# A transformer decoder layer on one core: other loads for the attention row maxima and the mask, two spread steps moved from TensorE to DMA and GpSimd, and the first half's last layer norm on ScalarE

## What is computed

```python
x = layernorm(x + self_attn(x))              # 16 heads of 8, one shared K and V of width 8
x = layernorm(x + cross_attn(x, ctx, mask))  # 16 heads of 8, scores -1e9 where mask == 0
x = layernorm(x + moe(x))                    # 8 experts 128x128, top 1, times its softmax weight

def self_attn(x):
    Q = heads(x @ Wq + bq); K = x @ Wk + bk; V = x @ Wv + bv
    attn = softmax(einsum('bhsd,btd->bhst', Q, K) / sqrt(8))
    return merge(einsum('bhst,btd->bhsd', attn, V)) @ Wo + bo
```

## Time and profile before

| | |
|---|---|
| median of 3 runs | 462.83 us (462.34 to 463.98) |
| the profiled execution | 465.59 us |
| its span in the trace | 464.0 us |
| mean granted TensorE clock | 0.97 of 2.4 GHz |
| busy: PE, DVE, ACT, POOL | 94%, 85%, 78%, 54% of the span |

### The profile page before, as it was taken

One profiled execution on the slowest core, in us unless ns is written; L12 is line 12 of the kernel. 1 busy time (PEld: TensorE's weight loads), 2 busy tenths in 40 slices (PEclk: granted clock), 3 DMA queues, 4 the chain that ended last, 5 costly groups with the idle time before them and its releaser, 6 DMA issues.

```text
span 464.0 us, 10785 instructions
## 1 busy us (share of the span) xinstructions
PE 438.2 (94%) x3873; PEld 177.2 (38%) x3873; DVE 395.0 (85%) x520; ACT 360.8 (78%) x708; POOL 248.7 (54%) x383
## 2 busy tenths in 40 slices
PE   7999999999889999999999999999999999999983
PEld 2543333333334333333344334333344443333441
DVE  5969989999788899899998999999999999941455
ACT  6338888889765877788868888889968888978723
POOL 4834889987897904042456644445447354320563
PEclk9879999999988999999999999999999999999978
DMA  6957967599770056221322346322212122110000
GB/s 164 342 121 230 310 201 293 182 364 350 249 316 1 15 114 98 64 68 42 92 71 69 115 92 105 89 72 60 83 45 69 49 72 70 47 32 23 4 24 26
DMA packets 24596, 56.08 MB, mean 121 GB/s; under 512 B 6442, under 2 KB 15928, under 8 KB 22492
## 3 DMA queue, kind: packets, MB, share of 16 engines
q0 software_dynamic: 7536, 37.91, 25.1%
q1 hardware_dynamic: 16424, 17.24, 14.3%
q10 hardware_dynamic: 580, 0.20, 0.2%
HBM read 45.60 MB, written 9.18 MB: 118 GB/s over the span
## 4 chain that ended last, share of the span: by engine, by line
PE 66%; DVE 12%; POOL 8%; DMA 7%; issue 4%; ACT 2%; SPq 0%; ACTq 0%; DVEq 0%; POOLq 0%
PE O L1512 25%; PE ST L1752 15%; PE RT L1745 7%; DVE mxs L944 7%; PE ST L1539 5%; POOL big L613 4%; DMA big<-in_mask 4%; PE RT L1527 3%; PE RT L1638 2%; DMA Qs<-mxr 2%; POOL big L622 2%; PE ST L1645 1%; PE O L1490 1%; DVE mxc L962 1%; PE RT L1608 1%
## 5 line engine op out<-in xcount | busy, mean ns | idle before, releaser
L1309 ACT ACTIVATE prob<-ST 128x512 f32<-128x512 f32 x512 | 279.5, 599 | 52.0 <-PE ST L1539 21.8
L944 DVE TENSOR_REDUCE mxs<-RT 128x2 f32<-128x1024 f32 x128 | 153.2, 1222 | 17.1 <-PE RT L1527 16.2
L961 DVE TENSOR_REDUCE mxc<-RT 128x2 f32<-128x1024 f32 x128 | 152.6, 1221 | 2.8 <-PE RT L1745 1.9
L1752 PE MATMUL ST<-Qs,Kc 64*128 64x512 f32 x320 | 117.4, 450 | 0.0
L1745 PE MATMUL RT<-Kr,Qs 64*128 64x512 f32 (+1 forms) x384 | 114.5, 398 | 0.0
L1512 PE MATMUL O<-prob,vst 128*9 128x256 f32 x1280 | 99.1, 381 | 1.7 <-ACT prob L1298 0.5
L1539 PE MATMUL ST<-Qs,Kself 64*128 64x512 f32 x256 | 96.2, 448 | 2.7 <-DMA Qs<-mxr 2.6
L1527 PE MATMUL RT<-Kself,Qs 64*128 64x512 f32 x256 | 89.8, 466 | 3.2 <-DVE mxs L944 2.0
L690 POOL DMA_DIRECT2D Kr<-kd x96 | 47.9, 503 | 72.7 <-PE RT L1745 57.6
L1512 PE MATMUL O<-prob,Vs 128*9 128x256 f32 x1024 | 80.5, 386 | 1.3 <-ACT osb L1246 0.3
L1752 PEld LDWEIGHTS ST<-Qs,Kc 64*128 64x128 f32 x320 | 50.4, 184 | 66.1 <-issue 38.3
(11 more groups left out here) (224 smaller groups left out, 331.8 us busy)
## 6 DMA issues: line engine op xcount, KB each, us to landing
big<-in_mask POOLq DMA_DIRECT2D x16, 1664.0 KB, 8.0
Kc<-kd POOLq DMA_DIRECT2D x64, 80.0 KB, 2.2
Kr<-kd POOLq DMA_DIRECT2D x64, 64.0 KB, 2.1
od_s<-osb SPq DMA_DIRECT2D x16, 128.0 KB, 2.6
kd<-Vx SPq DMA_DIRECT2D x4, 512.0 KB, 6.7
Qs<-qd_x SPq DMA_DIRECT2D x8, 256.0 KB
od_x<-osb SPq DMA_DIRECT2D x14, 128.0 KB, 1.7
Qs<-qd_s SPq DMA_DIRECT2D x12, 128.0 KB, 5.6
```

The lines of the kernel that those rows point to most:

```text
L944: freed(v.tensor_reduce(mxs[:, h % 2, c2, :].rearrange("p (f t) -> p f t", f=2)[:, :, q], bank[:, :].rearrange("p (f k) -> p f k", f=2), A ...
L961: return v.tensor_reduce(o[:, :, u % 4], src, AX.X, ALU.max)
L1309: freed(nc.scalar.activation(prob[:, s % SLOTS, f * HALF:(f + 1) * HALF], bank[:, :], ACT.Exp))
L1752: mm = mmul(o[:, :], Kc[STACK[f], b * P:(b + 1) * P], Qs[STACK[f], j, :], start=True, stop=not gen, skip_group_check=True)
```

## The change

Six things are done together.

1. `split_max` makes three bfloat16 parts by four POOL operations, where two fp32r parts were made by two. PE turns 24 rows by a bfloat16 identity (`identb`) in one pass; before it turned 16 rows as fp32. The rows in `Qs` are placed elsewhere (`MAXROWS`, `PRODUCTS`).
2. The splits of heads 3, 6 and 9 move from between L613 and L622 of mask tiles 3, 7 and 12 to ahead of the waits of those tiles.
3. Each mask tile is loaded by two DMAs of half the columns.
4. For "s1" and "x0" the spread is taken off PE and DVE: SP writes `rden` to memory and reads it back widened (`inverses_out`, `inverses_in`), and POOL multiplies (`norm_work`). Their products move to X(1, 9) and X(9, 9); what follows moves by one block or one step: turn, queries, logits, router weights, normalisation, and the stores and gathers of the queries.
5. In the tail POOL normalises no tile of the first half. It makes -mean/std (`shift`), and ACT normalises the four tiles after its last expert part and before it loads the table with Sqrt. DVE's statistics of that half move from ahead of the router's operations to between the two sums of experts. POOL waits for DVE's four normalised tiles before its sums of experts, where it waited after them.
6. The turn of the second half waits tile by tile, where it waited for all four.

The diff, cut to its core:

```diff
-MAX_AHEAD = {0: 0, 2: 2, 6: 5, 9: 7, 14: 10}
-MAX_BETWEEN = {0: 1, 3: 3, 4: 4, 7: 6, 10: 8, 12: 9}
+MAX_AHEAD = {0: 0, 2: 2, 3: 3, 6: 5, 7: 6, 9: 7, 12: 9, 14: 10}
+MAX_BETWEEN = {0: 1, 4: 4, 10: 8}
...
+            def inverses_out(a):
+                k = 1 if a == "s" else 2
+                sp.wait_ge(S("rden"), k + 1)
+                load(rd[a].rearrange("u q (h k) -> (u q h) k", k=P), rden[:, :], "rden_out")
+
+            def inverses_in(a):
+                k = 1 if a == "s" else 2
+                sp.wait_ge(S("rden_out"), 16 * k)
+                for q in range(4):
+                    w, r = slice((q % 2) * 256, (q % 2 + 1) * 256), 64 * (q // 2)
+                    load(rdenw[r:r + 64, w], rd[a][:, q, :].unsqueeze(1).to_broadcast([8, DH, 256]), "rden_in")
...
-                pool.dma_start(maskI[m % 2], t["mask"][q * P:(q + 1) * P, w * HALFT:(w + 1) * HALFT]) \
-                    .then_inc(S(f"mask_in{m % 2}"), 16)
+                for c in range(0, HALFT, HALFT // 2):
+                    pool.dma_start(maskI[m % 2][:, c:c + HALFT // 2],
+                                   t["mask"][q * P:(q + 1) * P, w * HALFT + c:w * HALFT + c + HALFT // 2]) \
+                        .then_inc(S(f"mask_in{m % 2}"), 16)
...
-                g_.tensor_copy(mxh[:, :, 0, :], parts).then_inc(S("mx_part"), 1)
+                step(g_.tensor_copy(mxh[:, :, 0, :], parts))
+                step(g_.tensor_tensor(mxl[:, :, :], parts, mxh[:, :, 0, :], ALU.subtract))
+                g_.tensor_copy(mxh[:, :, 1, :], mxl[:, :, :]).then_inc(S("mx_part"), 1)
                 pool.wait_ge(S("mx_part"), G + 1)
-                g_.tensor_tensor(mxh[:, :, 1, :], parts, mxh[:, :, 0, :].bitcast(F32), ALU.subtract) \
+                g_.tensor_tensor(mxh[:, :, 2, :], mxl[:, :, :], mxh[:, :, 1, :], ALU.subtract) \
                     .then_inc(S("mx_split"), 1)
...
-                if j == 1:
+                if j in (1, 9):
+                    k = 1 + j // 8
+                    pool.wait_ge(S("o_back"), 64 * (k + 1))
+                    pool.wait_ge(S("rden_in"), 64 * k)
+                    pool.wait_ge(S("rt_ready"), number(RT_AT, ("s0 y", "s1 y")[k - 1]))
+                    g_.tensor_tensor(aT[:, :], aTr[:, :], rdenw[:, :], ALU.mult).then_inc(S("o_scaled"), 1)
...
+            pool.wait_ge(S("xn"), 16)
             upper_experts(0, 2, 4)
-            pool.wait_ge(S("xn"), 16)
...
-            for q in range(4):
-                g_.tensor_scalar(outs[:, q, :], x[:, q, :], mv[:, q, 0:1], rstd[:, q:q + 1], ALU.subtract, ALU.mult) \
-                    .then_inc(S("out0_done"), 1)
+            step(g_.tensor_tensor(shift[:, :], mv[:, 0:4, 0], rstd[:, 0:4], ALU.mult))
+            g_.tensor_scalar(shift[:, :], shift[:, :], -1.0, None, ALU.mult).then_inc(S("first_std"), 1)
...
-                if s == X(1, 3):
-                    spread_rows("s", 1)
-                if s == X(1, 5):
+                if s == X(1, 9):
                     residual("s", 1)
...
+            act.wait_ge(S("first_std"), 1)
+            for q in range(4):
+                nc.scalar.activation(outs[:, q, :], x[:, q, :], ACT.Identity, bias=shift[:, q:q + 1],
+                                     scale=rstd[:, q:q + 1]).then_inc(S("out0_done"), 1)
...
-                pe.wait_ge(S("xn"), 4 * NORMS[a, ph])
+                if (a, ph) != ("x", 1):
+                    pe.wait_ge(S("xn"), 4 * NORMS[a, ph])
                 for q in range(4):
+                    if (a, ph) == ("x", 1):
+                        pe.wait_ge(S("xn"), 13 + q)
```

More of the change, by code:

```diff
@@ L37 @@
 STACK = (slice(0, 64), slice(64, P))
-PRODUCTS = (1, 64 + 3)
-MAXROWS = slice(0, 100, 33)
+PRODUCTS = (0, 96)
+MAXROWS = slice(36, 87, 10)
 PENROWS = (34, 65)
@@ L75 @@
 RT_JOBS = {76: ("s0 spread",), 79: ("s0 y",), 94: ("count",), 99: ("flags",), KV - 1: ("km",),
-           X(1, 3): ("s1 spread",), X(1, 5): ("s1 y",), X(9, 3): ("x0 spread",), X(9, 5): ("x0 y",),
-           X(10, 6): ("x0 logits",), X(14, 6): ("e0",), X(15, 1): ("e1",),
+           X(1, 9): ("s1 y",), X(9, 9): ("x0 y",),
+           X(11, 6): ("x0 logits",), X(14, 6): ("e0",), X(15, 1): ("e1",),
            STEPS: ("x1 spread", "x1 y", "x1 logits", "e2", "e3", "u7")}
 ST_JOBS = {66: ("bias",), 86: ("s0 turn",), 88: ("s0 q",), KV: ("vm",),
-           X(2, 3): ("s1 turn",), X(2, 6): ("s1 q",), X(10, 3): ("x0 turn",),
+           X(3, 3): ("s1 turn",), X(3, 6): ("s1 q",), X(11, 3): ("x0 turn",),
            STEPS: ("c0", "u0", "u1", "b0", "u2", "u3", "x1 turn", "u4", "c1", "u5", "b1", "u6")}
@@ L251, in decoder_layer @@
         qd = {a: dram(f"qd_{a}", [2, DH, HEADS, Q]) for a in "sx"}
+        rd = {a: dram(f"rd_{a}", [8, 4, 256]) for a in "sx"}
         kd, pd = dram("kd", [HEADS, PROD, KPAD]), dram("pd", [1, KUSE])
@@ L358, in o_back @@
                     sp.wait_ge(S(f"o_in{par}"), 16 * (4 * (k - 1) + units // 2))
-                if k > 1:
-                    before = ("s0", "s1", "x0")[k - 2]
-                    sp.wait_ge(S("rt_free"), number(RT_AT, before + " spread"))
+                if k == 2:
+                    sp.wait_ge(S("rt_free"), number(RT_AT, "s0 spread"))
+                if k > 2:
+                    sp.wait_ge(S("o_scaled"), k - 2)
                 g0 = 8 * ph
@@ L390, in gather_x_queries @@
                     sp.wait_ge(S("xq_in"), 80 * ph)
-                load(Qs[MAXROWS, 8 * ph:8 * ph + 8, :].bitcast(F32).rearrange("o h q -> o (h q)"), zerof[:, :], "xq_in")
+                load(Qs[MAXROWS, 8 * ph:8 * ph + 8, :].bitcast(F32).rearrange("o h (t q) -> o (h t) q", q=P),
+                     zerof[0:6, :].unsqueeze(1).to_broadcast([6, 32, P]), "xq_in")
                 for k in parts:
@@ L889, in _ @@
                 mark(v.tensor_reduce(rowc[:, f, 1:2], ident[:, r + 2 * DH:r + PROD], AX.X, ALU.add))
-                mark(v.tensor_tensor(rowc[:, f, 2:3], ident[:, 66 * f:66 * f + 1], ident[:, 66 * f + 33:66 * f + 34],
-                                     ALU.add))
+                r = MAXROWS.start + 3 * MAXROWS.step * f
+                mark(v.tensor_reduce(rowc[:, f, 2:3], ident[:, r:r + 21:10], AX.X, ALU.add))
                 mark(v.tensor_reduce(rowc[:, f, 3:4], parts[:, :, 0, :], AX.XY, ALU.add))
@@ L1186, in _ @@
             normalised(x, 1, "xn")
-            dve.wait_ge(S("bias_in"), 1)
-            statistics(0, "f_var")
             router_max(1)
@@ L1191, in _ @@
             lower_experts(2)
+            dve.wait_ge(S("bias_in"), 1)
+            statistics(0, "f_var")
             lower_experts(3)
@@ L1487, in turn_max @@
                 pe.wait_ge(S("mx_split"), G + 1)
-                rows = mxh[:, :, :, :].bitcast(F32).rearrange("p f k t -> p (f k t)")
-                if bank is None:
-                    mm = mmul(O[0:16, 256:256 + P], rows, ident[:, :], start=False, stop=False, skip_group_check=True)
-                else:
-                    mm = nc.tensor.transpose(ST[bank][0:16, 0:P], rows, ident[:, :])
+                if G == 0:
+                    pe.wait_ge(S("identb_made"), 1)
+                o = O[0:24, 256:256 + P] if bank is None else ST[bank][0:24, 0:P]
+                mm = mmul(o, mxh[:, :, :, :].rearrange("p f k t -> p (f k t)"), identb[:, :], start=bank is not None,
+                          stop=bank is not None, skip_group_check=True)
                 mm.then_inc(S("mx_turned"), 1)
@@ L1605, in project_out @@
                 o = rt_place(f"{a}{ph} y")
-                pe.wait_ge(S("rt_free"), number(RT_AT, f"{a}{ph} spread"))
+                if NORMS[a, ph] in (2, 3):
+                    pe.wait_ge(S("o_scaled"), NORMS[a, ph] - 1)
+                else:
+                    pe.wait_ge(S("rt_free"), number(RT_AT, f"{a}{ph} spread"))
                 for q in range(4):
```

66 lines of the change are left out of this document (35 added, 31 removed).

## The result

The changed kernel takes 467.16 us (median of 4, 466.02 to 470.97), the kernel before 462.58 (4 runs, 459.35 to 463.98). The ratio is 1.0105, 95% interval 1.0056 to 1.0154. The forecast was 460.3 with a range of 455.0 to 466.0: the kernel was to get faster and got slower, and the time lies outside the range. The profiled execution took 467.30, span 465.6, close to its median; that of before had lain 3.0 above its median, which turns out to matter.

What follows compares the result with a forecast made beforehand. PE was taken as the bound nearly everywhere, POOL's list up to head 10's split in self-attention. +5.6 − 1.7 − 2.5 − 3.9 = −2.5 took the median from 462.83 to 460.3 us, range 455.0 to 466.0.

Steps and rivals of the forecast that it cites:

- Part 1: Self-attention: added load issues and split operations lengthen POOL's list up to the split of head 10, +5.6 us.
- The lower bound of 0: POOL in self-attention: the added 10.8 us of work fit its 10.45 idle, so the split of head 10 comes no later.
- Part 2: Self- and cross-attention: PE's turns of row maxima take one pass, not two, −1.7 us in sum.
- Part 3: Cross-attention: two halves' spreads leave PE and DVE, 1.15 to 1.40 us saved per half, −2.5 us in sum.
- Part 4: Tail: DVE's tiles without POOL beside them, tile-by-tile turn, logits and experts at full clock, −3.9 us in sum.
- rival 2: Self-attention: PE also waits for splits of heads 5 and 7, the clock falls more often; 465.5 us, chance 0.16.
- Rival 1: Self-attention: POOL's additions are hidden in waits, head 10's split ends no later than 134.9; 454.7 us, chance 0.15.
- rival 3: Mask loads in self-attention: half tiles land 1.0 us later and hold POOL up; 465.3 us, chance 0.11.
- rival 4: Tail: the clock still drops because PE waits for ACT's copy and DVE's tiles; 462.6 us, chance 0.10.

Runs made afterwards that it cites:

- spreads_alone: The kernel before with only the two spreads moved off PE to DMA and POOL; ratio 0.9955 to the kernel before.
- stats_before_experts: Kernel before plus the change's spreads and tail, head 10's split ahead of POOL's two copies, DVE's statistics ahead of the first sum of experts; ratio 0.9852.
- tiny_second_load: The changed kernel with whole-tile mask loads and a second 2 KB load per tile that nothing waits for; ratio 1.0115 to the kernel before.
- after_again: The changed kernel run once more, unaltered, for a second profile; ratio 1.0104 to the kernel before.

## Why the prediction was wrong, point by point

- **Part 1, +5.6.** The mechanism was right, the size too small; this is the first step that failed. Split 10 ended 8.8 later, not 5.6. Work and the short gaps between operations came out as summed: 80.1 + 3.1 = 83.2, against 82.0 + 1.5 = 83.5. Two terms were too small. The waits took 3.1 where 1.6 were kept, 2.37 of it for one tile's load. And the list started 2.0 later: head 3 at 57.4, where the working took 55.4 from the trace of before and let nothing in the change reach that far back. Why the start is late is open; before itself has head 3 at 53.6 in its second profile. The lower bound of 0 took all 10.45 of idle time as room for 10.8 of work; in the changed kernel 6.2 of the list are still idle, half of it in the short gaps.
- **Part 2, −1.7.** Right where it can be read: the turn takes 0.15, and cross is 1.0 shorter with it (196.9 to 195.9; forecast 1.2). The 0.9 of the six turns in self can't be told: from split 10 to head 16 it takes 75.4 and 72.8 in the two profiles of before, 74.0 and 73.7 with the change.
- **Part 3, −2.5.** Right in kind, 1.75 in size. The price of 1.15 to 1.40 per half was that of the PE and DVE rows; a half gave 0.87. Where the rest goes is open: in spreads_alone a block with the product still takes 13.97, where 12.61 is plain.
- **Part 4, −3.9.** The second step that failed. −2.8 of it was the difference between half and full clock in one execution. The sum was made against that execution (465.59) and taken off the median (462.83), though the stretch is in two of four profiles of the old tail only. Measured alone, the tail is worth 1.4 us (0.1 to 2.7). The statistics were priced at +0.4 in a wait that shrinks; they cost DVE all of it, and POOL's last sums came 1.86 too late because of their place, as stats_before_experts shows.
- **The sum from the runs:** +8.5 (split 10, both profiles of either kernel), −1.0 turns, −1.75 spreads, −1.4 tail: +4.4, where 4.6 was measured between the medians. Against the forecast the four terms are 2.9, 0.7, 0.75 and 2.5 worse, so Parts 1 and 4 turned the sign. The terms are places in profiles and one ratio, each known to a microsecond or so; that they meet so closely is in part luck.
- **Rivals.** Of rival 2, given 0.16, the signs came: waits of PE at heads 5 and 7, each followed by half clock. Its price did not. The stretches were 3.4 us long, not 6.83, and POOL waited 0.4 in all for the row maxima behind the list's start, where the rival had 2.6 behind each stretch. So that its 465.5 lies near the measured time is luck. Rival 1 is refuted by the list, rival 3 by tiny_second_load, rival 4 by the tail's full clock.
- **Readings.** Of the 80 points that the earlier trace rows lists PE has 60, three quarters and not two thirds. The earlier trace rows holds loads of keys of 64 and 32 KB; those of 80 KB are not in it. ACT's four tiles took 0.41 each, not 0.3. None of these moved the sum.

## What to carry to other kernels

Count the issues of an engine that starts DMAs as work on its list: here each cost 0.50 to 0.60 us from 2 KB to 1664 KB, and one more per mask tile, 11 of the 16 on the list that bounds, cost 0.5% of the kernel alone and 1.2% on top of the rest of the change. Do not count all idle time of a list as room: here 10.8 us of work met 10.45 of idle, and 6.2 stayed idle. And before a stretch at half clock is counted as a gain, look at a second profile: here it was in two of four.

## What was not expected of the hardware

One DVE operation of 128 x 22 took from 0.23 to 3.34 us in different executions. In the changed kernel's first profile:

```profile
133.63 3.34 DVE L1180 COPY downx<-down 128x22 f32<-128x22 f32 x1
```

```profile
133.95 2.97 POOL L641 TENSOR_SCALAR big<-big 128x3328 uint8<-128x3328 uint32 x1
```

It ends at 136.97, POOL's operation at 136.92. In after_again the same copy met only the end of such an operation, which ran to 132.41, and ended at 132.45:

```profile
L1180 DVE COPY downx<-down 128x22 f32<-128x22 f32 x1 | 0.2, 229 | 0.0
```

```profile
130.44 1.97 POOL L650 TENSOR_TENSOR big<-big 128x832 int32<-128x832 int32 x1
```

In every profile of these kernels the copy ends 0.03 to 0.05 us behind a POOL operation on `big`. The row maximum of head 10 and PE behind it (2.56 us idle at 138.21) were late by this in the first of the two; the split of head 10 gained nothing where they were not, since PE then waited 6.83 for it at the turn. The same shows in the tail: L1120 took 0.93 at 447.73 and ended at 448.66, with POOL's sum L873:

```profile
447.34 1.26 POOL L873 TENSOR_TENSOR x<-x,big 128x512 f32<-128x512 f32 x1
```

The page "SBUF — State Buffer" of the Trainium skill, section "SBUF: two separate sides", says that DVE and POOL share a pair of ports as an exclusive lock: an operation of POOL, or one of DVE in a 2-port mode or with two inputs in SBUF, holds it for the whole instruction if it starts first, and the other blocks. These rows agree in that the small operation lasts until the large one ends. Who had the lock first they do not all show: in the first row the copy begins 0.32 ahead of POOL's operation, while POOL issues a load, and still waits for its end. The earlier trace rows and the changed tail fit too: DVE's four tiles took 2.36 beside POOL's sums and 1.12 without them.
